# Cross-attention with an expert layer: TensorE issues two attention slots as one group, and the rough scores keep their place behind each slot's scores

## What is computed

```python
q = (x @ Wq).reshape(B, Nq, h, dh)
k = (context @ Wk).reshape(B, Nk, h, dh)
v = (context @ Wv).reshape(B, Nk, h, dh)
scores = jnp.einsum('bqhd,bkhd->bhqk', q, k) * scale
attn = jax.nn.softmax(scores, axis=-1)
out = jnp.einsum('bhqk,bkhd->bqhd', attn, v).reshape(B, Nq, h * dh)
return out @ Wo + bo
```

## Time and profile before

| | |
|---|---|
| median of 3 runs | 1677.63 us (1676.56 to 1679.77) |
| the profiled execution, its time | 1673.04 us |
| the profiled execution, its span | 1671.3 us |
| TensorE matmuls busy | 1492.7 us, 89% of the span |
| VectorE busy | 976.4 us, 58% |
| ScalarE busy | 682.7 us, 41% |
| GpSimd busy | 913.2 us, 55% |

### The profile page before, as it was taken

The page is one execution under the profiler, slowest core; times in us unless marked ns, Lnnn a source line. Parts: engine busy times, 40 slices in busy tenths (PEclk is TensorE's granted clock), DMA queues, the critical chain, the costliest instruction groups (busy, mean ns, idle before and its releaser), DMA issues. The chain is left out here.

```text
span 1671.3 us, 25423 instructions
## 1 busy us (share of the span) xinstructions
PE 1492.7 (89%) x9169; PEld 884.5 (53%) x9169; DVE 976.4 (58%) x1670; ACT 682.7 (41%) x800; POOL 913.2 (55%) x417
## 2 busy tenths in 40 slices
PE   4989999999999999999999999999978138888883
PEld 3644444445444544444444444444377128878883
DVE  7555666666665666666566666666246635555651
ACT  3234444444444444444344444454431105444350
POOL 2125665575565566566556656666732213666663
PEclk7989999999999999999999999999979559998997
DMA  7420010001001001000100100011062502343322
GB/s 215 176 92 8 20 47 14 14 20 53 14 14 49 20 15 52 15 14 20 49 14 20 47 14 20 20 39 58 26 224 94 180 14 69 85 88 77 78 33 21
DMA packets 90796, 89.48 MB, mean 54 GB/s; under 512 B 25904, under 2 KB 70985, under 8 KB 90569
## 3 DMA queue, kind: packets, MB, share of 16 engines
q1 hardware_dynamic: 68657, 79.16, 14.3%
q0 software_dynamic: 22016, 8.69, 3.5%
HBM read 59.43 MB, written 27.99 MB: 52 GB/s over the span
## 5 line engine op out<-in xcount | busy, mean ns | idle before, releaser
L688 POOL TENSOR_TENSOR acc_p<-acc_p,x_in 128x1024 f32<-128x1024 f32 x224 | 535.3, 2390 | 342.2 <-ACT x_in L734 332.2
L92 DVE TENSOR_REDUCE mx_part<-ps_m 128x1 f32<-128x512 f32 x744 | 478.4, 684 | 290.9 <-PE ps_m L80 287.3
L734 ACT ACTIVATE x_in<-ps_s 128x1024 f32<-128x1024 f32 x384 | 393.3, 1024 | 434.2 <-PE ps_s L604 433.1
L616 PE MATMUL ps_o<-x_in,v 128*64 128x512 f32 x1664 | 448.8, 618 | 0.0
L599 PE MATMUL ps_s<-q,k 64*128 64x512 f32 x1248 | 203.5, 429 | 0.0
L599 PEld LDWEIGHTS ps_s<-q,k 64*128 64x128 f32 x1248 | 103.6, 186 | 149.3 <-ACT x_in L734 103.9
L604 PE MATMUL ps_s<-m_rows,ones_row 64*128 64x512 f32 x832 | 166.5, 393 | 0.0
L616 PEld LDWEIGHTS ps_o<-x_in,v 128*64 128x64 f32 x1664 | 82.5, 135 | 139.1 <-issue 137.5
L599 PEld LDWEIGHTS ps_s<-q_hi,k_hi 64*128 64x128 f32 x416 | 38.8, 183 | 150.4 <-ACT x_in L734 101.0
L624 POOL TENSOR_TENSOR acc_p<-acc_p,acc_d 128x1024 f32<-128x1024 f32 x32 | 76.2, 2380 | 75.2 <-DVE acc_d L688 75.2
L1262 POOL DMA_INDIRECT xg<-table,idx_g x40 | 50.2, 1255 | 110.2 <-DVE idx_g L1252 100.4
(11 more groups left out here) (245 smaller groups left out, 2325.6 us busy)
## 6 DMA issues: line engine op xcount, KB each, us to landing
w_in<-in_w SPq DMA_DIRECT2D x16, 1024.0 KB, 8.4
v_st<-rec_scr SPq DMA_DIRECT2D x64, 128.0 KB, 2.9
o_scr<-v_st SPq DMA_DIRECT2D x32, 256.0 KB, 2.1
v_scr<-c_in SPq DMA_DIRECT2D x13, 512.0 KB, 2.6
v<-v_scr SPq DMA_DIRECT2D x8, 832.0 KB, 5.2
ot<-o_scr SPq DMA_DIRECT2D x2, 2048.0 KB, 11.2
x_in<-in_x SPq DMA_DIRECT2D x4, 512.0 KB, 7.6
x<-in_x SPq DMA_DIRECT2D x4, 512.0 KB, 10.3
```

The source lines that it names most:

```text
L92: dve.tensor_reduce(part[:, j // S.MF, j % S.MF:j % S.MF + 1], bank[:, 0:S.MC], AX.X, ALU.max).then_inc(G.rough_used[hd], 1)
L616: last = pe.matmul(ps_o[hd * HP:hd * HP + DH, :], v[b][:, s, hd * DH:(hd + 1) * DH], probs[:, g % RING, hd * QC:(hd + 1) * QC], start=(s = ...
L688: eng.tensor_tensor(acc, other, probs[:, (u * KT + t) % RING, :], ALU.add).then_inc(done, 1)
L734: act.activation(probs[:, g % RING, :], ps_s[:, g % 2, :], ACT.Exp, bias=G.pad_bias[:, 0:1] if s == KT - 1 else 0.0, scale=SCALE).then_inc ...
```

## The change

`pe_pair` now goes through the slots two at a time. It issues the scores of slot g, its rough pair, the scores of slot g+1, its rough pair, then the products with the values of both (of slots g-2 and g-1), and then the small jobs of both. Where slot g holds the last tile's product of a unit (`changes`, at g = 14 and 40 of a pair's 52), the first product with the values keeps its old place. ScalarE takes both exponentials before the small copies. The small jobs move to slots that never share a group, the transposed maxima go from slot 11 to slot 9, and `MAHEAD` goes from 3 to 5, so that five rough jobs stand ahead of the first slot.

```diff
-PROJ_SLOTS = (4, 6, 8, 10)
-DEN_SLOT, MROW_SLOT = 3, 11
+PROJ_PLACES = ((0, 4), (0, 6), (0, 10), (1, 2), (1, 5), (1, 7), (1, 11), (2, 4))
+DEN_SLOT, MAX_SLOT, MROW_SLOT = 3, 8, 9
-MAHEAD = 3
+MAHEAD = 5
...
         def pe_pair(pe, p, b, first=False, last=False):
-            for g in range(SLOTS):
...
-                pe_scores(pe, g, u, s, b, unit)
-                if job:
...
-                    pe_rough(pe, 1 - b if other else b, (u + ahead) % UNITS, j, (unit + ahead) * MJOBS + j)
...
-                    pe_pv(pe, (g - LAG) % SLOTS, slot - LAG, p * UNITS + (g - LAG) // KT, p if g >= LAG else p - 1,
...
+            for g in range(0, SLOTS, 2):
+                changes = g % KT == LAG - 1
+                scores(g)
+                rough(g)
+                if changes:
+                    values(g)
+                scores(g + 1)
+                rough(g + 1)
+                if not changes:
+                    values(g)
+                values(g + 1)
+                small(g)
+                small(g + 1)
...
         def act_pair(act, p, b, first=False, last=False):
...
+            for g in range(0, SLOTS, 2):
...
+                exponentials(g)
+                output(g)
+                exponentials(g + 1)
+                output(g + 1)
+                copies(g)
+                copies(g + 1)
...
         def dve_pair(dve, p, b, first=False, last=False):
...
-                if s == KT - MAHEAD and not (last and u == UNITS - 1):
+                if s == MAX_SLOT and not (last and u == UNITS - 1):
...
-                if s - 1 in PROJ_SLOTS and u < 2 and not last:
+                if divmod(g - 2, KT) in PROJ_PLACES and not last:
```

More of the change, by code:

```diff
@@ L423 @@
 POOL_TILES = (0, 1, 4, 5, 6, 8, 9, 10, 11)
-PROJ_SLOTS = (4, 6, 8, 10)
-DEN_SLOT, MROW_SLOT = 3, 11
+PROJ_PLACES = ((0, 4), (0, 6), (0, 10), (1, 2), (1, 5), (1, 7), (1, 11), (2, 4))
+DEN_SLOT, MAX_SLOT, MROW_SLOT = 3, 8, 9
 REC_SLOT, NORM_SLOT = 7, 12
-MAHEAD = 3
-PROJ_JOBS = 2 * len(PROJ_SLOTS)
+MAHEAD = 5
+PROJ_JOBS = len(PROJ_PLACES)
 def wait_for(eng, s, count):
@@ L457, in phase_attention @@
     ND, NPL = len(DVE_TILES) - 1, len(POOL_TILES) - 1
-    assert SLOTS % RING == 0 and KT == MJOBS and UNITS == S.QB
+    assert SLOTS % RING == 0 and SLOTS % 2 == 0 and KT == MJOBS and UNITS == S.QB
     with ExitStack() as ctx:
@@ L501, in x_wait @@
         def x_wait(pe, p, u, s, last):
[L503 to L511, removed]
+            first = isinstance(p, int) and p == 0
+            users = [((a, DEN_SLOT), den_copied, UNITS * p + a) for a in range(1 if first else 0, UNITS)]
+            users += [((a, MROW_SLOT), mrow_ready, UNITS * p + a + 2) for a in range(UNITS)]
+            users += [(at, stage_lo, PROJ_JOBS * p + n + 1) for n, at in enumerate(PROJ_PLACES) if not last]
+            users = [((-1, MROW_SLOT), mrow_ready, UNITS * p + 1)] + [x for x in users if x[0] < (u, s)]
+            at, copied, count = max(users, key=lambda x: x[0])
+            pe.wait_ge(copied, count)
         def pe_rough(pe, b, c, j, count):
@@ L548, in block_of @@
         def block_of(n):
-            return n % 2 == 0, n // 2
+            return n >= UNITS, n % UNITS
         def pe_proj(pe, n, pair):
@@ L691, in pe_pair, with rough @@
         def pe_pair(pe, p, b, first=False, last=False):
-            for g in range(SLOTS):
+            def rough(g):
                 u, s = divmod(g, KT)
-                unit, slot = p * UNITS + u, p * SLOTS + g
                 job = rough_job(u, s, last)
-                if not (first and g < 2):
-                    pe.wait_ge(exp_done, slot - 1)
-                pe_scores(pe, g, u, s, b, unit)
                 if job:
@@ L703, in pe_pair, with scores, values, small @@
                         pe.wait_ge(stage_lo, PROJ_JOBS * (p + 1))
-                    pe_rough(pe, 1 - b if other else b, (u + ahead) % UNITS, j, (unit + ahead) * MJOBS + j)
+                    pe_rough(pe, 1 - b if other else b, (u + ahead) % UNITS, j, (p * UNITS + u + ahead) * MJOBS + j)
+            def scores(g):
+                u, s = divmod(g, KT)
+                if not (first and g < 2):
+                    pe.wait_ge(exp_done, p * SLOTS + g - 1)
+                pe_scores(pe, g, u, s, b, p * UNITS + u)
+            def values(g):
                 if not (first and g < LAG):
-                    pe_pv(pe, (g - LAG) % SLOTS, slot - LAG, p * UNITS + (g - LAG) // KT, p if g >= LAG else p - 1,
+                    pe_pv(pe, (g - LAG) % SLOTS, p * SLOTS + g - LAG, p * UNITS + (g - LAG) // KT, p if g >= LAG else p - 1,
                           b if g >= LAG else 1 - b)
+            def small(g):
+                u, s = divmod(g, KT)
+                unit = p * UNITS + u
                 if s == DEN_SLOT and not (first and u == 0):
@@ L710, in pe_pair @@
                     pe_den(pe, (u - 1) % UNITS, unit - 1)
-                if s in PROJ_SLOTS and u < 2 and not last:
+                if (u, s) in PROJ_PLACES and not last:
                     x_wait(pe, p, u, s, last)
-                    pe_proj(pe, u * len(PROJ_SLOTS) + PROJ_SLOTS.index(s), p + 1)
+                    pe_proj(pe, PROJ_PLACES.index((u, s)), p + 1)
                 if s == MROW_SLOT and not (last and u == UNITS - 1):
@@ L716, in pe_pair, with exponentials @@
                     pe_maxt(pe, unit + 1)
+            for g in range(0, SLOTS, 2):
[11 more added lines that the diff above has]
+                small(g + 1)
         def act_pair(act, p, b, first=False, last=False):
-            for g in range(SLOTS):
+            def exponentials(g):
                 u, s = divmod(g, KT)
[L721 to L724, removed]
+                slot = p * SLOTS + g
                 if not (first and g < RING):
@@ L735, in act_pair, with copies @@
                                bias=G.pad_bias[:, 0:1] if s == KT - 1 else 0.0, scale=SCALE).then_inc(exp_done, 1)
-                if s == LAG - 1 and not (first and u == 0):
-                    act_o(act, unit - 1)
+            def copies(g):
+                u, s = divmod(g, KT)
+                unit = p * UNITS + u
                 if s == DEN_SLOT and not (first and u == 0):
                     act_den(act, unit - 1)
-                if s in PROJ_SLOTS and u < 2 and not last:
-                    n = u * len(PROJ_SLOTS) + PROJ_SLOTS.index(s)
+                if (u, s) in PROJ_PLACES and not last:
+                    n = PROJ_PLACES.index((u, s))
                     act_proj(act, n, 1 - b, PROJ_JOBS * p + n)
@@ L744, in act_pair, with output @@
                     act_mrow(act, unit + 1)
+            def output(g):
+                u, s = divmod(g, KT)
+                if s == LAG - 1 and not (first and u == 0):
+                    act_o(act, p * UNITS + u - 1)
+            for g in range(0, SLOTS, 2):
+                if last and g == KT + 1:
+                    act.wait_ge(wo_loaded, 16)
+                    act.activation(G.wo_hi[:], wo_in, ACT.Copy).then_inc(wo_hi_done, 1)
+                exponentials(g)
[4 more added lines that the diff above has]
+                copies(g + 1)
         def dve_pair(dve, p, b, first=False, last=False):
@@ L756, in dve_pair @@
                     add_tile(dve, DVE_TILES.index(s - 1) - 1, u, unit, slot - s, dve=True)
-                if s - 1 in PROJ_SLOTS and u < 2 and not last:
-                    n = u * len(PROJ_SLOTS) + PROJ_SLOTS.index(s - 1)
+                if divmod(g - 2, KT) in PROJ_PLACES and not last:
+                    n = PROJ_PLACES.index(divmod(g - 2, KT))
                     dve_proj(dve, n, 1 - b, PROJ_JOBS * p + n)
```

## The result

The changed kernel takes **1726.74 us** (median of 4 runs, 1723.76 to 1726.89) against 1677.1 us (4 runs): ratio 1.030, interval 1.0282 to 1.0317. It is 49.6 us slower; the forecast was 1734.5, in a range of 1706 to 1756.

A forecast was written before the change was run, and what follows sets the result against it. TensorE's stream of matmuls was taken to bound the attention. 118.6 us of stall less 65 us of gain, +2.7 for rough jobs and +0.9 in the last unit gave +57 us on 1677.6: 1734.5 us, range 1706 to 1756.

The forecast's parts named there:

- What bounds the kernel: Attention: it lasts as long as TensorE's stream of matmuls; a change is worth what it takes out or puts in.
- What the grouping removes: Each group of two slots: two changes of matmul shape go, 0.34 us saved in 192 groups, 65 us.
- What it adds: Second rough pair of a group: TensorE waits for VectorE to release head 1's bank, 0.725 us; 118.6 us together.
- The two places in the kernel before: Loop's second turn and prologue: maxima's end to head 1's load 0.06 us, load to next matmul about 0.43.
- Which groups stall: Seven head pairs: 20 groups of 0.725 us and two of 0.48 each; none with `changes` or slot 7, units 1 and 3.
- the last paragraph: What the changed profile would show: groups of 5.1 us, and of 4.4 at slot 7 of units 1 and 3.
- The sum: Whole kernel: 118.6 us of stall less 65 of gain, plus small additions, +57 us, giving 1734.5 us.
- the jobs less what leaves the loop: Ahead of the first slot: two more rough jobs, less two rough pairs that leave the loop, +2.7 us.
- I cost all of these at 0: Moved work on ScalarE, VectorE and GpSimd, small jobs, copies and transposed maxima: all fit, 0 us.
- the faster case: Second rough pair of each group: no stall but the gain stays, 1617 us; chance 0.05.
- that rival: VectorE falls behind as its tile sums meet GpSimd's work, 2.56 us instead of 1.22: 1780 us; chance 0.1.
- The clock: Attention: TensorE's clock falls through half-microsecond pauses; a tenth at half clock, about 55 us more, 1790; chance 0.05.

The follow-up runs named there:

- first experiment: Changed kernel with each group's first rough pair moved ahead of the scores of its slot: 1665.5 us, ratio 0.9937 to the kernel before.
- third: Changed kernel with a group's second rough pair moved between its two products with values: 1673.7 us, ratio 0.9991 to the kernel before.
- fourth experiment: Changed kernel with TensorE's slots issued singly again, everything else as changed: 1674.9 us, ratio 0.9999 to the kernel before.
- first kernel with the maxima first: First rough pair ahead of its group's scores, plus VectorE's maxima ahead of tile sums and projections' low parts, against the changed kernel: 1683.8 us, ratio 1.0050.
- changed kernel with the same edit: Changed kernel with only VectorE's order changed, maxima ahead of tile sums and projections' low parts: 1770.8 us, ratio 1.0570.
- the last kernel: Changed kernel plus first rough pair first, low parts of first slots behind maxima, normalisation in slot 10, `MAHEAD = 4`, `MAX_SLOT = 9`: 1642.3 us, ratio 0.9803.

## Why the prediction was right

**What bounds the kernel.** Right: TensorE's stream. By the starts of its matmuls in the two profiles, 4.3 us are lost up to the first product with the values, 43.8 over the seven head pairs behind it and 2.7 in the last one and after it, together the 50.7 by which the spans differ.

**What the grouping removes, 0.34 us a group.** Right. Without VectorE in the way a group took 4.40 us (first experiment), with the changes of shape back 4.73 (third). The estimate worked out from the Trainium skill (TensorEngine Tiling, "Key Properties", with the drain and the weight load of TensorE: Matmul & The Clock Gate) was 0.27; the measurement decides for 0.33.

**What it adds, 0.725 us a group.** Right in mechanism and size: values 2.20 us behind the first rough pair (2.21 said), groups of 5.11. The two places in the kernel before that gave 0.06 and 0.43 carried this term. Halving the maxima took 0.54 us out of each full group.

**Which groups stall.** Nearly right. The group with slot 7 of units 1 and 3 doesn't stall, but it takes 4.72 us, not 4.4. I had forgotten in the last paragraph that its small products cost 0.25 in any kernel; it did not enter the sum. The group with slot 7 of units 0 and 2 takes 5.23, where 4.40 + 0.25 + 0.48 = 5.13 was worked out.

**The sum.** Undisturbed, a head pair takes 146.51 us (254.11 to 400.62, first products with the values) against 139.55 (242.62 to 382.17): +6.96, where the prediction has (108.2 - 57)/7 = 7.3. Over seven that is 49, 2 less than said. About that much is a small wait of the kernel before: at the four places of a head pair where a unit changes, two slots took 4.81 us there instead of 4.73, and the changed kernel has no such wait. The first scores start 3.1 us later, counted from the first rough job (2.7 said for the jobs less what leaves the loop).

**What was mis-sized: "I cost all of these at 0", the loop's turns.** Two of the seven intervals hold a turn back to the loop's start. Before they took 142.86 and 144.36 us, 3.3 and 4.8 more than the others; now 148.12 and 148.29, 1.6 and 1.8 more. That gave back 4.7 us, most of the 7 by which the forecast was too high. About 1 of the 4.7 is not the turn but the half clock behind the second one, described under the fourth experiment. The timeline of the changed kernel there:

```profile
540.42 0.50 PE L597 MATMUL ps_s<-q_hi,k_hi 64*128 64x512 f32 x2 [1.54 <-issue]
540.48 1.23 DVE L686 TENSOR_TENSOR acc_d<-acc_d,x_in 128x1024 f32<-128x1024 f32 x1 [1.42 <-issue]
...
541.44 0.40 PE L80 MATMUL ps_m<-k_hi,q_hi 64*128 64x512 f32 x2
...
541.87 2.57 DVE L92 TENSOR_REDUCE mx_part<-ps_m 128x1 f32<-128x512 f32 x4 [0.17 <-PE ps_m L80]
...
542.61 1.09 PE L80 MATMUL ps_m<-k_hi,q_hi 64*128 64x512 f32 x2
```

Both engines come back from the turn 1.5 us late. Before, VectorE was late once more, with its first maxima of the turn at 520.87, and TensorE stood behind it; here its maxima start 0.43 after the rough pair, and the rest of that wait lies in a group that stalls anyway. The first experiment fits: its group at the head pair's end waits for VectorE in any case, and the intervals with a turn are only 0.3 to 0.4 us longer than the others. That it is this is read from the profiles, not tested.

**The rivals.** The stall was there, so the faster case fell. VectorE did not fall behind in the changed kernel (its first maxima of a group start 0.43 after the rough pair), but the other half of that rival came true: 50 of its 96 tile sums met a sum of GpSimd, where 3 did before; 19 of these took over 1.3 us, the longest 3.17. VectorE did fall behind as soon as the stall was taken away. The clock stayed at 1.00 in the changed kernel, from 105 to 1200 us, through pauses of half a microsecond and two of 1.6 us; the prediction took the 1.00 of 95 us for the whole attention of the kernel before, which has one stretch at half clock. The Trainium skill's TensorEngine Tiling, "PSUM Bottleneck", points at the right place, the engine that empties the bank. But this was not a limit of how much VectorE can empty: it is busy 58% in both kernels, and the plain groups of the first experiment hold the same work without the wait. What decided was how far apart two uses of one bank lie.

**Where I was wrong: the expectations.** The first experiment was expected at 1608 with a remark of up to 1620; the step that failed was to take VectorE's time from durations alone (2.58 of 4.40 us), not from what stands ahead of the maxima in its queue. The next step failed in the opposite way: moving that work behind the maxima delayed something that TensorE waits for too.

## What to carry to other kernels

When work is moved together on the engine that sets the time, look for pairs of its instructions that hand a single buffer back and forth with a slower engine, and compare their new distance with the other engine's full turn: 1.165 us against 1.78 decided the result here. Put such instructions at the two ends of the group and not behind each other; that alone was worth 61 us. Before changing the other engine's order, list who waits for each thing that stands behind the one you move forward.

## What was not expected of the hardware

- A sum of two SBUF tiles on VectorE took up to 3.39 us (first kernel with the maxima first, at 220.37), and a normalisation 2.08 (first experiment), where they overlapped one of GpSimd's sums of 2.38 us. Without such an overlap every tile sum in these traces took 1.15 to 1.23 and every normalisation 0.68. The maxima, which read PSUM, stayed at 665 to 694 ns in all ten traces that have them in full. The Trainium skill's SBUF: State Buffer ("SBUF: two separate sides") says that of a VectorE operation with two SBUF inputs and a GpSimd operation that reads SBUF, the later one waits until the other has finished. The trace agrees: the sum at 288.39 started 0.22 behind GpSimd's at 288.17 and ended 1.07 behind its end, and the longest, 3.39, is not much under 1.22 + 2.38 = 3.60.
- A pause of over 3 us in TensorE's matmuls was followed by matmul steps of 0.43 instead of 0.23 us; in the window 285 to 310 us of that kernel the mean granted clock was 0.86. But the clock does not follow the pause alone: of the seven pauses of 3.13 us in that kernel six were followed by half the clock, of seven of 2.4 us in the changed kernel with the same edit four, and of the two at the turns of the kernel before only the one of 1.81 us, not the one of 1.43. The pauses of the changed kernel, of half a microsecond and two of 1.6, left it at 1.00 over 1095 us.
- At a turn of the loop TensorE's matmuls pause for 1.4 to 1.8 us (kernel before and changed kernel), and VectorE for about as long. The interval with the turn was longer than the others by 0.3 us at the least (first experiment) and by 4.9 at the most (the last kernel), so the kernel around the turn decides what it costs.
